# A selective-scan layer with a mixture of experts on one core: the causal mask of G moved from VectorE to GpSimd for 14 pairs of 16

## What is computed

```
v = (v - dt*A*y + dt*u*Bv) / denom
y = y + dt*v + dt*u*By
o = y . Cy + v . Cv          # per token
```

## Time and profile before

| what | value |
|---|---|
| median of 3 runs | 566.69 us |
| lowest, highest | 564.38, 570.17 us |
| the profiled execution, its own time | 568.01 us |
| its span, first to last instruction | 566.3 us |
| mean granted TensorE clock | 0.904 of full speed |
| VectorE busy | 488.0 us (86%) |
| TensorE matmul busy | 436.1 us (77%) |
| ScalarE busy | 263.5 us (47%) |
| GpSimd busy | 201.8 us (36%) |

### The profile page before, as it was taken

One profiled execution on the slowest core, in us unless ns is written; L12 is line 12 of the kernel. 1 busy time (PEld: TensorE's weight loads), 2 busy tenths in 40 slices (PEclk: granted clock), 3 DMA queues, 4 the chain that ended last, 5 costly groups with the idle time before them and its releaser, 6 DMA issues.

```text
span 566.3 us, 9333 instructions
## 1 busy us (share of the span) xinstructions
PE 436.1 (77%) x3220; PEld 354.5 (63%) x3220; DVE 488.0 (86%) x1219; ACT 263.5 (47%) x461; POOL 201.8 (36%) x265
## 2 busy tenths in 40 slices
PE   2970019997979928898989937988789956998997
PEld 1850018885856717686757726777675745786886
DVE  5599998989899999989799999898989997788543
ACT  1651224553565624454547632545537542443463
POOL 2000016768510007667530006676640005767100
PEclk9986557999999968998979976999999996998999
DMA  7400000000000010000000000000000000000000
GB/s 223 141 1 0 0 1 2 1 2 1 1 1 1 2 37 2 1 1 1 2 0 0 3 19 1 2 2 1 1 2 0 1 19 2 2 2 1 0 11 11
DMA packets 8433, 7.05 MB, mean 12 GB/s; under 512 B 1593, under 2 KB 7618, under 8 KB 8258
## 3 DMA queue, kind: packets, MB, share of 16 engines
q1 hardware_dynamic: 8386, 6.46, 3.8%
HBM read 5.41 MB, written 1.05 MB: 11 GB/s over the span
## 4 chain that ended last, share of the span: by engine, by line
PE 41%; DVE 32%; POOL 12%; issue 8%; ACT 5%; DMA 0%; SPq 0%; DVEq 0%; POOLq 0%; ACTq 0%
PE HB L523 6%; DVE tp L1158 4%; PE BC L569 4%; POOL vt L1591 4%; DVE hist L1158 3%; PE OO L551 3%; PE RR L551 3%; DVE mm L1273 3%; PE HB L472 3%; PE HB L531 3%; DVE pr L1273 3%; POOL big L1588 3%; PE GV L591 2%; POOL rinv L1607 2%; DVE mm L1311 2%
## 5 line engine op out<-in xcount | busy, mean ns | idle before, releaser
L1588 POOL TENSOR_TENSOR big<-mm 128x256 f32<-128x256 f32 x64 | 50.0, 781 | 289.9 <-DVE mm L1311 289.9
L569 PE MATMUL BC<-xnT,winT 128*128 128x128 f32 x512 | 78.1, 301 | 76.9 <-DVE mm L1311 76.8
L569 PEld LDWEIGHTS BC<-xnT,winT 128*128 128x128 f32 x512 | 69.3, 210 | 83.1 <-DVE mm L1311 79.7
L1591 POOL TENSOR_TENSOR vt<-mm 128x256 f32<-128x256 f32 x64 | 57.9, 904 | 0.0
L854 ACT ACTIVATE pr<-hist 128x512 f32<-128x512 f32 x32 | 34.0, 1113 | 49.8 <-DVE hist L1158 49.8
L523 PE MATMUL HB<-xnT,w 128*128 128x512 f32 x108 | 55.0, 637 | 2.3 <-ACT gtm L939 1.3
L1158 DVE TENSOR_TENSOR tp<-big,hist 128x256 f32<-128x256 f32 x124 | 51.8, 418 | 1.4
L876 ACT ACTIVATE big<-GV 128x256 f32<-128x256 f32 x60 | 23.0, 384 | 63.8 <-PE GV L594 62.3
L591 PE MATMUL GV<-big,vt 128*128 128x128 f32 x256 | 45.0, 302 | 9.3 <-POOL vt L1591 9.3
L1309 DVE TENSOR_TENSOR mm<-BC,pr 128x512 f32<-128x512 f32 x64 | 44.2, 690 | 5.7
L591 PEld LDWEIGHTS GV<-big,vt 128*128 128x128 f32 x256 | 36.9, 208 | 14.9 <-POOL vt L1591 12.0
(11 more groups left out here) (204 smaller groups left out, 1061.0 us busy)
## 6 DMA issues: line engine op xcount, KB each, us to landing
xr<-in_x SPq DMA_DIRECT2D x4, 256.0 KB, 4.8
winT<-in_w_inT SPq DMA_DIRECT2D x1, 1024.0 KB, 6.3
w<-in_rw SPq DMA_DIRECT2D x1, 1024.0 KB
out<-xr SPq DMA_DIRECT2D x3, 256.0 KB, 2.3
taps<-in_dw_wT SPq DMA_DIRECT2D x1, 512.0 KB, 3.6
w<-in_sw SPq DMA_DIRECT2D x2, 128.0 KB
out<-xr SPq DMA_DIRECT2D x2, 128.0 KB, 1.8
winT<-in_w_inT SPq DMA_DIRECT2D x1, 130.0 KB, 2.5
```

What stands on the lines that cost most here:

```text
L569: last = pe.matmul(b[:, j * TS:(j + 1) * TS], winT[:, col:col + NS], xt, start=True, stop=True)
L1588: pool.tensor_tensor(wt[q % 8][:], m[:, 0], m[:, 3], ALU.add)
L1591: pool.tensor_tensor(vt[q % 2][:], view(m, 5 * TS, (-3 * TS, 2), (1, TS)), view(m, 3 * TS, (TS, 2), (1, TS)), ALU.subtract).then_inc(wv_do ...
```

## The change

For the first 14 pairs of a group (k = 0 to 13) the mask goes to GpSimd. GpSimd has no way to PSUM here, so ScalarE copies G and V^T in one instruction of 384 columns instead of V^T alone, and GpSimd zeroes the wrong side of G in place with `affine_select`. G and V^T of a pair therefore lie side by side in SBUF: `wide` takes the place of `big` and `gtm` at the same total size. For the last two pairs of a group VectorE masks out of PSUM as before. In the last tile, which has no V^T, ScalarE now copies G of its first two pairs alone (128 columns), where it copied nothing.

```diff
+BY_DVE = 2
+COPIED = NT * NH - BY_DVE
...
+def masked_before(q):
+
+    g, k = divmod(q, KP)
+    return BY_DVE * g + max(k - (KP - BY_DVE), 0), (KP - BY_DVE) * g + min(k, KP - BY_DVE)
...
-        big = sb("big", 128, 16 * 2 * TS)
+        wide = sb("wide", 128, (16 * 2 + 8) * TS)
+        big = wide[:, 0:16 * 2 * TS]
...
-        vts = [part(8 + i) for i in range(8)]
-        gtm = sb("gtm", TS, 8 * TS)
-        gts = [gtm[:, i * TS:(i + 1) * TS] for i in range(8)]
+        gvs = [wide[:, (16 + 3 * i) * TS:(19 + 3 * i) * TS] for i in range(8)]
+        gts = [t[:, 0:TS] for t in gvs]
+        vts = [t[:, TS:3 * TS].rearrange("p (i n) -> p i n", i=2) for t in gvs]
...
                 # gv, TensorE
                 if q >= 2:
-                    pe.wait_ge(gm_done, q - 1)
-                    pe.wait_ge(vt_done, min(q - 1, TURNED))
+                    pe.wait_ge(vt_done, min(q - 1, COPIED))
+                    if masked_before(q - 1)[0] > masked_before(q - 2)[0]:
+                        pe.wait_ge(gm_done, masked_before(q - 1)[0])
...
                 # tail, TensorE
-                pe.wait_ge(gm_done, NH * (tile + 1))
+                by_dve, by_pool = masked_before(NH * (tile + 1))
+                if by_dve:
+                    pe.wait_ge(gm_done, by_dve)
+                pe.wait_ge(gs_done, by_pool)
...
                 # vt_copy, ScalarE
-                act.activation(vts[q % 8][:], GV[q % 2][:, V_COLS].rearrange("p (i n) -> p i n", i=2), ACT.Copy)\
-                    .then_inc(vt_done, 1)
+                first = TS if q % KP >= KP - BY_DVE else 0
+                cols = slice(first, 3 * TS if q < TURNED else TS)
+                act.activation(gvs[q % 8][:, cols], GV[q % 2][:, cols], ACT.Copy).then_inc(vt_done, 1)
...
                 # VectorE, step k
-                    if 0 <= k - MASK < KP:
+                    if KP - BY_DVE <= k - MASK < KP:
                         causal_g(KP * g + k - MASK)
...
+            def upper_zero(q):
+
+                pool.wait_ge(vt_done, q + 1)
+                pool.affine_select(out=gts[q % 8], in_=gts[q % 8], compare_op=ALU.is_ge, fill=0.0, base=0,
+                                   pattern=[[1, TS]], channel_multiplier=-1).then_inc(gs_done, 1)
...
                     if k < KP:
                         wv(KP * g + k)
+                    if 0 <= k - MASK < KP - BY_DVE:
+                        upper_zero(KP * g + k - MASK)
```

More of the change, by code:

```diff
@@ L207, in build @@
         w9T = x1[0:NX].rearrange("p i d -> p (i d)")
-        hh = [t[:].rearrange("p (i t) -> p i t", i=2) for t in (gtm, sqs)]
+        hh = [t[:].rearrange("p (i t) -> p i t", i=2) for t in (wide[:, 32 * TS:40 * TS], sqs)]
         hh_half = [t.rearrange("p (i t) -> p i t", i=2) for t in (hist[:, 3 * 4 * TS:4 * 4 * TS], sqs[:, 4 * TS:8 * TS])]
@@ L244, in build @@
             ("bc_ready", "sq_done", "vc_done", "mul_done", "wv_done"))
-        gv_done, gm_done, vt_done, ub_done, gate_done = (sem(s) for s in
-            ("gv_done", "gm_done", "vt_done", "ub_done", "gate_done"))
+        gv_done, gm_done, gs_done, vt_done, ub_done, gate_done = (sem(s) for s in
+            ("gv_done", "gm_done", "gs_done", "vt_done", "ub_done", "gate_done"))
         r_done, tail_done, rts_done, rt_done, z_done, y1_done, op_done, x2_done, xi_done = (sem(s) for s in
@@ L267, in entry @@
             comp = lambda role: f if role == "x" else 1 - f
-            return view(big, ((2 * f + comp(operand)) * 2 + comp(row)) * DS * KP, (DS, KP), (1, DS))
+            return view(wide, ((2 * f + comp(operand)) * 2 + comp(row)) * DS * KP, (DS, KP), (1, DS))
         scr = lambda f, i: view(mm[f], i * DS * KP, (DS, KP), (1, DS))
@@ L544, in expert_out @@
                 elif u == EARLY:
-                    pe.wait_ge(gm_done, NT * NH)
-                    pe.wait_ge(vt_done, TURNED)
+                    pe.wait_ge(gm_done, BY_DVE * NG)
+                    pe.wait_ge(vt_done, COPIED)
                 yb = banks_of(u)[n % 2]
@@ L616, in tail @@
                 pe.wait_ge(ub_done, tile + 1)
-                pe.wait_ge(vt_done, min(NH * (tile + 1), TURNED))
+                pe.wait_ge(vt_done, min(NH * (tile + 1), COPIED))
                 if tile:
@@ L969, in _ @@
                             act.preload_act_table_set("natural_log_exp_and_others")
-                    if 0 <= k - COPIES < KP and KP * g + k - COPIES < TURNED:
+                    if 0 <= k - COPIES < KP and KP * g + k - COPIES < COPIED:
                         vt_copy(KP * g + k - COPIES)
@@ L1256, in step_products @@
                 now = (i - 1) % RING * ST if i else 0
-                step_op(view(tp, 0, (2 * KP, 8), (1, 2 * KP)), view(big, i, (DS, 8 * KP), (0, 2)),
+                step_op(view(tp, 0, (2 * KP, 8), (1, 2 * KP)), view(wide, i, (DS, 8 * KP), (0, 2)),
                         view(hist if i else start, now, (2 * KP, 4), (0, 2), (1, 2 * KP)), ALU.mult)
@@ L1295, in causal_g @@
                 dve.wait_ge(gv_done, q + 1)
-                dve.wait_ge(vt_done, min(q + 1, TURNED))
+                dve.wait_ge(vt_done, min(q + 1, COPIED))
                 if q >= 8:
```

## The result

The changed kernel takes 570.44 us in the median of 17 runs (568.53 to 572.82), the one before 568.13 (564.22 to 570.17) beside it. The ratio is 1.0061, with a 95% interval of 1.0043 to 1.0078. It is slower by 2.3 us by the medians and by 3.5 us by the ratio, within the 1% that was forecast and inside the range, but on the losing side and by seven to ten times the +0.35 us of the sum. (Of the 3.4 us between the forecast 567.0 and 570.44, 1.4 are the kernel before itself, which the prediction took at 566.69.) The profiled execution took 572.82 us with a span of 571.1, against 568.01 and 566.3. It is the slowest of the 17, while that of the kernel before lies at its median, so the profiles show more of a loss, 4.8 us, than the typical run has.

A forecast was written before the change was run, and what follows sets the result against it. The chain of waits, led by TensorE (41%) with VectorE at 32%, was taken as the bound. Terms 0.25 + 2 x (-0.2) + 0 + 0.5 = +0.35 us on 566.69 gave 567.0 us, range 562.0 to 572.3.

The forecast's parts named there:

- GpSimd's mask at 0.25 us from start to start: Each of 56 added affine_selects costs 0.25 us, mostly hidden in GpSimd's pauses, except straight before a tile's ubar.
- ScalarE's copy at +106 ns: Copy widened from 256 to 384 columns: 106 ns more, 54 times; 6.3 us in all with the last tile, costed at nothing.
- The turns of the two engines: GpSimd and VectorE block each other: whoever has begun an instruction goes on to its end, the other waits.
- the unbroken stretches of TensorE: In the first three pair phases TensorE is never idle for 20.1, 13.9 and 14.0 us; VectorE's gains there go into waiting.
- signs of being wrong: Pair phases of groups 0 to 2 shorter by over 1 us each, or affine_select over 0.5 us in front of rinv.
- GpSimd becomes the bound: Rival, chance 0.09: 9 places ahead of ub or gate cost 0.78 us each, 7.0 us, giving 573.7.
- End part ... I take 0: From the unbroken stretch on, groups 0 to 2: the added mask before gate is hidden by the second scan; ends -0.4, +0.8.
- Groups 1 and 2, first part ... -0.2 for each: Up to the unbroken stretch: pair 8 hangs on ub, which ends 0.2 us earlier by no longer waiting behind xi.
- +0.25 was forecast: Group 0 up to the unbroken stretch: no mask on the chain, ubar(0) later by 0.25 us.
- VectorE is the bound after all: Rival, chance 0.13: a path beside the chain is only tenths shorter; 42 masks count 8.4 us, giving 558.3.
- the sum allowed 2.4: Most that VectorE's relief gives back: 1.2 us from six masks on the chain, 1.2 us from masks behind the stretches.
- Group 3: Three tiles get +0.25 us before their ub, the first cancelled by xi: +0.5 us, ends 0 and 2.3.

The follow-up runs named there:

- five masks: The changed kernel with the masks of pairs 11 to 15 of a group on VectorE and 11 on GpSimd: 565.57 us, 0.9965 of the kernel before.
- GpSimd's masks besides: The kernel before, with GpSimd also doing 56 affine_selects on two spare tiles at their places in the changed kernel: 567.60 us, ratio 0.9983.
- the spacer: The changed kernel, with VectorE also making pair 13's mask into an unread tile ahead of the first scan in groups 0 to 2: 564.36 us, 0.9912.
- quarters: The changed kernel with pair 13's mask back on VectorE and each scan cut into four of 128x256: 567.11 us, 0.9978 of the kernel before.
- three masks: The changed kernel with pair 13's mask back on VectorE, which masks pairs 13 to 15 of a group: 562.15 us, 0.988 of the kernel before.

## Why the prediction was right, and where it was wrong

The verdict (no change by 1%, in the range) was right, the reasons for it only in part. Two errors of opposite sign stood in the sum, 8.8 us lost at the scans and 4.0 gained elsewhere by the profiles, and that the difference stayed under 1% is luck.

**What held.** GpSimd's mask at 0.25 us from start to start, and hidden: 0.998 with all of them added to the kernel before. ScalarE's copy at +106 ns, hidden. The turns of the two engines, and the unbroken stretches of TensorE. VectorE's wait for the broadcast grew from 2.0 to 3.0 us, as it was to. Its busy time fell by 18.0 us and not by 10 to 16; 1.6 of these are the scans, recorded with 14.6 us in place of 16.2 as they no longer wait for GpSimd. Of the signs of being wrong, one came in part: the pair phases of groups 1 and 2 shortened by over 1 us, that of group 0 did not.

**"GpSimd becomes the bound"** had its price wrong: 0.78 us per mask is not what an `affine_select` costs. (By its own terms it would decide from 2.4 / 9 = 0.27 us on, not from 0.35.) But what it said in passing, that GpSimd's instructions stretch to 2.7 us beside a scan, is what cost the time, in `wt` and `vt` and not in a mask.

**The step that failed most: "End part ... I take 0".** I argued that the gate waits for the second scan whatever stands before it. That took it as given that GpSimd begins `wv` of pair 15 ahead of the first scan, as in the earlier trace rows. But this was so only because the mask of pair 13 stood between the products and the scan. Without it the scan is issued behind the products and starts 0.17 us ahead of GpSimd, which waits until they are complete. Two turns go to VectorE, and TensorE stands idle for 3.6 us: 2.83, 2.37 and 3.59 us over the long stretches, 2.45, 3.52 and 3.57 over the short distances, in place of 0 (upper end: 0.8 each). I had the rule and the rows and applied them to the instruction that is added, and not to the gap that the removed one leaves. The experiments show it from four sides: the mask put back (0.988), a useless one in its place (0.9912), the same order in the kernel before (1.0084), and shorter scans (0.991).

**The step that failed the other way: "Groups 1 and 2, first part ... -0.2 for each".** By pair 8 the changed kernel was 1.03 and 1.04 us ahead of the one before, counted from the group's first pair. I took the square that ended at 235.55 for the one that pair 8 needs. It is that of pair 9: `proj` of pair 8 stands ahead of `tail` in TensorE's step. The square of pair 8 is this, from the timeline of ScalarE in the kernel before:

```profile
230.41 0.58 ACT L870 ACTIVATE hist<-BC 128x512 f32<-128x512 f32 x1
```

It was ready 4.7 us before VectorE got to pair 8. So `ub` had no hold on pair 8, and VectorE's own time counted there, with some turns on top. In the changed kernel two small instructions, L1090 and L1093, take 0.17 us each at that place:

```profile
231.48 0.17 DVE L1090 TENSOR_TENSOR tf<-tf,dtbb 128x16 f32<-128x16 f32 x1
231.68 0.17 DVE L1093 TENSOR_SCALAR tf<-tf 128x16 f32<-128x16 f32 x1
```

In the kernel before they took 0.58 and 0.65 us, beside `ub` and the first sum of GpSimd. `ub` itself took 0.61 us, as forecast, but the power before it 2.13, so that `ub` ended 0.3 us later and not 0.2 earlier. The account does not hold for group 0: there pair 8 came 0.62 us later, where +0.25 was forecast, and the last pair at +0.03. What took and gave this was not found.

**The rival "VectorE is the bound after all"** (0.13) was the better half of the truth. With the order at the scan mended, four kernels came out 5 to 7 us under the one before (0.988 to 0.9912), where the sum allowed 2.4; on one chip, with five masks, it was 2.0. Counting masks on one chain gave too little. The likely reason is the one that the rival names, that a second path was only tenths longer; no run shows it by itself.

**Group 3** came to +0.31 us by its last pair, near the +0.5, but by luck: at pair 8 it was 0.71 us ahead. The 1.08 us that the changed kernel is faster behind it were not forecast; the stretch is as short (46.92) in the kernel before with GpSimd's masks besides, and 48.57 in the one with the spacer. What decides between these lengths was not found.

**Open:** how large the loss is in a run of the usual 570 us, as both profiles of the changed kernel are of runs near 572.9; why five masks on VectorE gave less than three; why quarters lost; and how large the relief is and how it divides among the groups (group 1 took 53.8 us in the profiled run of three masks, and 52.2 in that of the changed kernel).

## What to carry to other kernels

An instruction that is taken out has two effects: its time, and the gap that it made for others. Where two engines take turns at a shared resource and one of them holds it for 2 us at a time, ask which of them begins first, by how many nanoseconds, and whether the removed instruction was what decided; here a mask of 0.20 us was worth 2.5 to 3.6 us per group. And before a slack is read from a row, follow the program's order to make sure that it is the row of the same pair.

## What the runs showed of the hardware

- An instruction of GpSimd with one input waits its turn as well: the `affine_select` of 128x128 takes 0.29 us undisturbed, 1.21 beside a scan of 128x512 and 2.28 beside one of 128x1024. The Trainium skill ("GPSIMD Engine Reference", section "Specifications") names the contention; that a turn lasts until the other engine's instruction ends, these rows show: GpSimd's sum waits for a scan of 512 to its end (1.58 and 1.64 us) and for one of 1024 to its end (2.64 and 2.71).
- Undisturbed, the scan of 128x1024 takes 2.28 us; it is recorded with 2.84 and 2.56 when GpSimd has begun before it.
- A TensorE idle for 3.6 us came back at a granted clock of 0.53 over the next 6.2 us (changed kernel, group 1), and the answering stretch had 1.00 when it was idle for 0.2 us. The clock also fell without so long a wait: to 0.57 over 7.9 us in the kernel before with the mask behind the scan, where TensorE was busy for 7.2 us of these and for 1.9 of the 4 us from 158 to 162 us.
